# Unread matrix products in TensorE's waits, and weight remainders moved forward on VectorE, in a two-layer attention and expert kernel

## The chip, the cores and the metric

The kernel runs on one core of one Trainium2 chip. The time is device microseconds of one execution of the whole program, lower is better. The time before is the median of three runs, 1602.66 us (1599.79, 1602.66 and 1603.99).

## The reference, cut to what matters

4096 tokens (4 sequences of 1024) of 128 features pass through four blocks, each followed by a residual and a layer norm:

```python
x = _layernorm(x + _L0_attn_ref(x, ...))   # causal attention, 16 heads of 8, scores clipped to +-10
x = _layernorm(x + _L0_ffn_ref(x, ...))    # 8 experts, top 2: (silu(x W1) * (x W2)) W3, width 256
x = _layernorm(x + _L1_attn_ref(x, ...))   # full attention, 16 heads of 8, rotary embedding
x = _layernorm(x + _L1_ffn_ref(x, ...))    # 4 experts, top 2: gelu(x We1) We2, width 512
```

All of it is float32. Every expert is computed for every token and weighted by its gate.

## The kernel before

The five engines run their own programs and meet only at semaphores. The order of the stages is fixed: q, k and v of layer 0 (to about 31 us), causal attention of layer 0 (`pe_causal`, to about 301 us), the experts of layer 0 (`pe_end(.., 0)`, to about 702 us, which also makes q, k and v of layer 1), full attention of layer 1 (`pe_full`, to about 1357 us), the experts of layer 1 (`pe_end(.., 1)`).

**Experts of layer 0.** Tokens come in eight chunks of 512 (`CH`). A chunk has 16 steps (`SPC`). The work that prepares a chunk, its "front" (output projection, residual, norm, transposes, router), and the work that finishes one, its "back" (norm, rotation, q, k, v of layer 1), are spread over the steps beside the expert matmuls; the table `plan` says at which step each piece stands. For layer 0 the front's pieces are `o_turn` and `o_proj` at 1, `norm` at 3, `x_turn` at 4, `router` at 5. The very first front has no expert matmuls beside it: `pe_end`, `act_end` and `dve_end` call the 16 steps alone. In it VectorE divides the attention output by the row sums (`ot`, L1377), takes a reciprocal (L553), adds the residual (L1384), takes the statistics (L1284, L1287); GpSimd makes `rstd` of them with two small operations (L1518, L1519); VectorE normalises (`xs`, L1292); TensorE transposes `xs` (L946); ScalarE copies the result twice (`xt`, L1209, and its rounded half `x_hi`, L1210); TensorE computes the router (L1102), VectorE the remainder `x_lo` (L1401). Then the first expert matmuls start (L1031).

Float32 is made of rounded halves in the expert matmuls: a weight `w` is `w_hi + w_lo`. ScalarE rounds (`w_hi`, `w3_hi`), VectorE subtracts: `w_lo[0]` and `w_lo[1]` (L1486) after step `norm`, and `w3_lo` (L1490) after all 16 steps. `pe_first_hidden` waits for `w_lo`, `x_lo` and then `w3_lo`.

**The last back and the start of the full attention.** After the last chunk, 16 steps of back alone run (`pe_beside(.., 2 * B - 1, None, ..)`), with eight "pairs" between them (`pe_pair_beside_back`). A pair is two matmuls of 32 contracted rows and 512 columns into one slot of a ring of two (`max_pair`, L689); VectorE takes their row maxima (`negmax_h`, L808) and frees the slot. `pe_full` then issues pairs 8 to 27 alone (`first_pairs`), eight score matmuls (L703), and 16 rounds of 16 steps. A step has two parts, each with one pair, two scores and four value matmuls of 256 columns (`full_o`, L718); a score waits until ScalarE's exponential (L771) has emptied one of three banks.

Of the kernel before, what the change touches and what calls it, by code (L numbers as in the profile page):

```python
# [7 lines left out]
ALU = mybir.AluOpType  # L8
# [198 lines left out]
def build_program(nc, d, out):  # L207
    with ExitStack() as ctx:
# [548 lines left out]
        def pe_full(pe, L):  # L757
            for m in first_pairs(L):
                pe_pair(pe, L, 0, 0, m, m, m % 2)
            for e in range(HG * AHEAD):  # L760
                pe_score(pe, L, 0, 0, e)
            pe_full_round(pe, L, 0, 0, True)
            for i in range(1, NG):
                pe_full_round(pe, L, i, i % 2, i < NG - 1)
# [237 lines left out]
        EARLY_STEPS = {s: [n] for s, n in zip(EARLY, (plan[1].o_proj, plan[1].x_turn, plan[1].hidden, plan[1].router))}  # L1002
        RH_AT = 8
        n_exp = [E0, E1]

# [132 lines left out]
        def pe_chunk(pe, st, c, par, back, front, layer):  # L1138
            for n in range(SPC):
# [8 lines left out]
                pe_product(pe, st, c, n, layer)  # L1148

        def pe_first_hidden(pe, st, layer):  # L1150

            pe.wait_ge(w_lower, 2 * (layer + 1))
            for n in range(h_lead[layer]):
                pe_hidden(pe, st, 0, 0, n, layer)
            if layer == 0:
                pe.wait_ge(st.w3_lower, 1)
# [9 lines left out]
        def pe_end(pe, st, layer):  # L1166
            if layer == 0:
                for n in range(SPC):
                    pe_beside(pe, st, n, None, 0, 0, layer)
            else:  # L1170
                pe.wait_ge(st.gate_pre, 1)
# [6 lines left out]
            for n in range(SPC):  # L1178
                pe_beside(pe, st, n, 2 * B - 1, None, 0, layer)
                if layer == 0:  # L1180
                    pe_pair_beside_back(pe, layers[1], n)

# [287 lines left out]
        def dve_end(dve, st, layer):  # L1471
# [4 lines left out]
            for n in range(SPC):  # L1476
                dve_beside(dve, st, n, None, 0, 0, layer)
                if layer == 1 and n == plan[1].x_turn:
                    for k in range(2):
                        dve.wait_ge(raw_loaded[k], 32)  # L1480
                        nc.vector.tensor_copy(w_hi[k][:, :], w_raw[k][:, :]).then_inc(w_upper, 1)
                if n == (plan[0].norm, plan[1].x_turn)[layer]:

                    for k in range(2):
                        dve.wait_ge(w_upper, 2 * layer + k + 1)
                        nc.vector.tensor_tensor(w_lo[k][:, :], w_raw[k][:, :], w_hi[k][:, :].bitcast(F32),  # L1486
                                                ALU.subtract).then_inc(w_lower, 1)
            if layer == 0:
                dve.wait_ge(st.w3_upper, 1)
                nc.vector.tensor_tensor(w3_lo[:, :, :], w3[:, :, :], w3_hi[:, :, :].bitcast(F32),  # L1490
                                        ALU.subtract).then_inc(st.w3_lower, 1)
                dve.wait_ge(rope_loaded, 16 * 2)
# [359 lines left out]
```

## Time and profile before

| What | Value |
|---|---|
| median of three runs | 1602.66 us |
| profiled execution, its own time | 1611.3 us |
| its span, first to last instruction | 1609.5 us |
| TensorE busy | 1471.5 us (91%) |
| VectorE busy | 1400.4 us (87%) |
| ScalarE busy | 1202.9 us (75%) |
| mean granted TensorE clock | 0.952 |

### The profile page before, as it was taken

How to read it: one execution, taken by the hardware profiler on the slowest of the kernel's cores; microseconds unless marked ns; L12 is line 12 of the kernel's file. 1: busy time of each engine (PE TensorE's matmuls, PEld its weight loads, DVE VectorE, ACT ScalarE, POOL GpSimd, SP SyncE). 2: the span in 40 equal slices, each digit the busy share in tenths (PEclk: the TensorE clock that was granted, in tenths of full speed). 3: DMA queues.
4: the chain of work that ended last, by engine and by line, in shares of the span. 5: the costliest groups of instructions: out<-in, count | busy, mean ns of one | idle time of the engine just before them, and what ended most of it. 6: DMA issues, size and time to landing. Idle time of an engine off the chain costs nothing.

```text
span 1609.5 us, 32282 instructions
## 1 busy us (share of the span) xinstructions
PE 1471.5 (91%) x11200; PEld 797.1 (50%) x11200; DVE 1400.4 (87%) x2394; ACT 1202.9 (75%) x1897; POOL 307.5 (19%) x325
## 2 busy tenths in 40 slices
PE   7989898689999999969999999999999998999996
PEld 4333333377777777623333333333333334777775
DVE  5899999878888988887999999999999973788886
ACT  4999999644445454417999999999999986777775
POOL 0000000234455454420000000000000001234333
PEclk9899999799999998966999999999999997999999
DMA  6636432131224431111111111111111110211211
GB/s 203 203 106 182 120 102 86 49 107 40 96 93 127 128 108 66 66 41 51 46 37 37 46 45 38 42 37 36 37 36 36 37 32 28 69 56 63 75 56 40
DMA packets 71026, 116.76 MB, mean 73 GB/s; under 512 B 23808, under 2 KB 33920, under 8 KB 70272
## 3 DMA queue, kind: packets, MB, share of 16 engines
q1 hardware_dynamic: 70912, 115.21, 23.5%
q8 instruction: 75, 1.23, 0.3%
q14 instruction: 39, 0.32, 0.1%
HBM read 73.49 MB, written 41.16 MB: 71 GB/s over the span
## 4 chain that ended last, share of the span: by engine, by line
PE 61%; DVE 15%; ACT 10%; issue 10%; POOL 1%; DMA 1%; DVEq 0%; ACTq 0%; SPq 0%; POOLq 0%
PE full_o L718 14%; PE hid_pair L1031 12%; PE max_pair L689 11%; ACT cprobs L491 7%; PE bank L1134 7%; DVE negmax_h L808 5%; PE score L703 4%; PE causal_o L463 3%; PE triple L447 2%; PE bank L1066 2%; ACT o_sb L779 1%; DVE st L1284 1%; PE hid_pair L952 1%; PE bank L1094 1%; DVE hid_lo L1458 1%
## 5 line engine op out<-in xcount | busy, mean ns | idle before, releaser
L771 ACT ACTIVATE probs<-score 128x512 f32<-128x512 f32 x1024 | 546.6, 596 | 89.5 <-PE score L703 69.5
L808 DVE TENSOR_REDUCE negmax_h<-max_pair 128x2 f32<-128x1024 f32 x512 | 588.6, 1216 | 24.9 <-PE max_pair L689 24.8
L718 PE MATMUL full_o<-probs,v_st 128*32 128x256 f32 x4096 | 337.9, 403 | 17.7 <-ACT o_sb L779 17.7
L703 PE MATMUL score<-q_st,k_st 32*128 32x512 f32 x1024 | 319.9, 510 | 2.6 <-ACT probs L771 2.6
L689 PE MATMUL max_pair<-k_st,q_st 32*128 32x512 f32 x1024 | 264.7, 515 | 12.2 <-DVE negmax_h L808 10.8
L491 ACT ACTIVATE cprobs<-triple 128x1536 f32<-128x1536 f32 x192 | 258.4, 1713 | 5.2 <-PE triple L447 5.2
L689 PEld LDWEIGHTS max_pair<-k_st,q_st 32*128 32x128 f32 x1024 | 97.8, 188 | 236.7 <-DVE negmax_h L808 179.9
L1240 ACT ACTIVATE act_s<-hid_pair 128x512 f32<-128x512 f32 x128 | 76.7, 599 | 149.5 <-PE hid_pair L1031 149.5
L1031 PE MATMUL hid_pair<-x_hi,w_hi 128*128 128x512 f32 x384 | 171.3, 446 | 1.8 <-DVE x_lo L1401 1.0
L521 DVE TENSOR_SCALAR cprobs<-cprobs 128x1536 f32<-128x1536 f32 (+6 forms) x272 | 160.7, 618 | 2.9 <-ACT cprobs L491 2.9
L463 PE MATMUL causal_o<-cprobs,v_st 128*32 128x512 f32 (+3 forms) x1536 | 156.2, 502 | 2.2 <-DVE cprobs L521 2.2
L718 PEld LDWEIGHTS full_o<-probs,v_st 128*32 128x32 f32 x4096 | 83.3, 109 | 150.0 <-issue 94.5
L703 PEld LDWEIGHTS score<-q_st,k_st 32*128 32x128 f32 x1024 | 141.6, 187 | 28.8 <-ACT probs L771 19.5
L1031 PE MATMUL hid_pair<-x_lo,w_hi 128*128 128x512 f32 x384 | 154.6, 403 | 0.0
L1031 PE MATMUL hid_pair<-x_hi,w_lo 128*128 128x512 f32 x384 | 154.3, 402 | 0.0
L447 PE MATMUL triple<-q_st,k_st 32*128 32x512 f32 (+3 forms) x768 | 101.5, 429 | 28.7 <-ACT cprobs L491 26.0
L447 PEld LDWEIGHTS triple<-q_st,k_st 32*128 32x128 f32 x768 | 47.6, 186 | 135.5 <-ACT cprobs L491 127.1
L1248 ACT ACTIVATE hid_hi<-hid_pair,be 128x512 fp32r<-128x512 f32 x128 | 89.0, 695 | 24.9 <-PE hid_pair L1031 17.9
L1134 PE MATMUL bank<-hid_hi,w_hi 128*128 128x512 f32 x256 | 101.9, 398 | 1.4 <-DVE qk_lo L1436 1.3
L1134 PE MATMUL bank<-hid_hi,w_lo 128*128 128x512 f32 x256 | 101.4, 396 | 0.0
L568 POOL COPY v_st<-v_all 128x256 f32<-128x256 f32 x32 | 12.7, 400 | 434.6 <-PE causal_o L463 246.3
L520 DVE SCALAR_TENSOR_TENSOR cprobs<-cprobs,bound 128x256 f32<-128x256 f32 (+4 forms) x160 | 92.3, 577 | 3.9 <-ACT cprobs L491 2.5
(157 smaller groups left out, 2001.8 us busy)
## 6 DMA issues: line engine op xcount, KB each, us to landing
gate_all<-gate_scr SPq DMA_DIRECT2D x48, 512.0 KB, 4.3
o_scr<-o_sb SPq DMA_DIRECT2D x64, 256.0 KB, 2.1
k_st<-k_scr SPq DMA_DIRECT2D x64, 128.0 KB, 2.8
q_st<-q_scr SPq DMA_DIRECT2D x128, 64.0 KB, 2.5
k_st<-k_scr SPq DMA_DIRECT2D x64, 96.0 KB
q_st<-q_scr SPq DMA_DIRECT2D x64, 96.0 KB
q_scr<-qk_hi SPq DMA_DIRECT2D x18, 256.0 KB, 4.6
k_scr<-qk_hi SPq DMA_DIRECT2D x18, 256.0 KB, 4.5
```

The costliest lines, as they stand in the source:

```text
L447: last = nc.tensor.matmul(triple[n % 2][:, bk, off:off + w], k_st[p][rows, kt * P:(kt + 1) * P], q_st[p][rows, q0:q0 + w], start=True, sto ...
L463: last = nc.tensor.matmul(causal_o[qc][SLOT * j:SLOT * (j + 1), c0:c0 + w], v_st[p][:, kt, j, :], cprobs[at % CP][:, bk, off:off + w], sta ...
L491: nc.scalar.activation(cprobs[n % CP][:, :, :], triple[n % 2][:, :, :], ACT.Exp, scale=SCALE).then_inc(L.exp_done, 1)
L520: nc.vector.scalar_tensor_tensor(edge, edge, float(np.exp(-CLIP)), limit, ALU.max, ALU.min)
L521: ins = nc.vector.tensor_scalar(plain, plain, float(np.exp(-CLIP)), float(np.exp(CLIP)), ALU.max, ALU.min)
L689: last = nc.tensor.matmul(ring[slot][:, k, :], q_st[p][rows, qt * P:(qt + 1) * P], k_st[p][rows, half * CH:(half + 1) * CH], start=True, s ...
L703: nc.tensor.matmul(sbank[L.score_bank(e)][:, :], k_st[p][rows, kt * P:(kt + 1) * P], q_st[p][rows, q0:q0 + w], start=True, stop=True, tile ...
L718: last = nc.tensor.matmul(full_o[SLOT * j:SLOT * (j + 1), cols], v_st[p][:, kt, j, :], probs[s % NP][:, j, cols], start=(kt == 0 and part ...
L771: nc.scalar.activation(probs[s % NP][:, L.HEADS[j], :], sbank[L.score_bank(e)][:, :], ACT.Exp, scale=SCALE).then_inc(L.exp_done, 1)
L808: nc.vector.tensor_reduce(negmax_h[:, qt // TPC, half, heads[0]:heads[1] + 1:2, qt % TPC], ring[slot][:, :, :], AXX, ALU.max, negate=True) ...
L1031: last = nc.tensor.matmul(hbank[2 * k + n % h_banks[layer]], w[:, slice_of(n)], x[:, :], start=(a == 0), stop=(a == 2))
L1134: last = nc.tensor.matmul(y_bank[e % 2], w, x, start=(f == 0 and a == 0), stop=(f == per - 1 and a == 2))
```

## The change

A helper issues products that nobody reads: the 128x128 identity times the first columns of the table `rope_a`, float32. They are put at five places in TensorE's program: one of 512 columns at the start of the first front, three after its step 1, one after its step 4; two after step 1 and two after step 2 of the last back; one of 256 columns after each of the 20 pairs of `first_pairs`. On VectorE, `w_lo[0]` is computed after step 0 of the first front (behind `ot` and the reciprocal), `w_lo[1]` after step 1 (behind the statistics), `w3_lo` after step 3 (behind `xs`).

```diff
@@ pe_full
             for m in first_pairs(L):
                 pe_pair(pe, L, 0, 0, m, m, m % 2)
+                pe_keep_busy(bank[0], 1, CH // 2)
@@
+        BUSY_FRONT, BUSY_BACK = {1: 3, 4: 1}, {1: 2, 2: 2}
@@
+        def pe_keep_busy(to, many, cols):
+
+            for _ in range(many):
+                nc.tensor.matmul(to[:, 0:cols], ident[:, :], rope_a[:, 0:cols], start=True, stop=True)
@@ pe_end
             if layer == 0:
+                pe.wait_ge(rope_loaded, 16 * 2)
+                pe_keep_busy(hbank[0], 1, CH)
                 for n in range(SPC):
                     pe_beside(pe, st, n, None, 0, 0, layer)
+                    if n in BUSY_FRONT:
+                        pe_keep_busy(hbank[0], BUSY_FRONT[n], CH)
@@
                 if layer == 0:
                     pe_pair_beside_back(pe, layers[1], n)
+                    if n in BUSY_BACK:
+                        pe.wait_ge(st.v_saved, 2 * B - 1)
+                        pe_keep_busy(bank[2], BUSY_BACK[n], CH)
@@ dve_end
-                if n == (plan[0].norm, plan[1].x_turn)[layer]:
-
-                    for k in range(2):
+                if layer == 0 and n == plan[0].norm:
+                    dve.wait_ge(st.w3_upper, 1)
+                    nc.vector.tensor_tensor(w3_lo[:, :, :], w3[:, :, :], w3_hi[:, :, :].bitcast(F32),
+                                            ALU.subtract).then_inc(st.w3_lower, 1)
+                for k in ((0,) if n == plan[0].o_turn - 1 else (1,) if n == plan[0].o_proj else ()) if layer == 0 else (
+                        (0, 1) if n == plan[1].x_turn else ()):
                         dve.wait_ge(w_upper, 2 * layer + k + 1)
                         nc.vector.tensor_tensor(w_lo[k][:, :], w_raw[k][:, :], w_hi[k][:, :].bitcast(F32),
                                                 ALU.subtract).then_inc(w_lower, 1)
             if layer == 0:
-                dve.wait_ge(st.w3_upper, 1)
-                nc.vector.tensor_tensor(w3_lo[:, :, :], w3[:, :, :], w3_hi[:, :, :].bitcast(F32),
-                                        ALU.subtract).then_inc(st.w3_lower, 1)
                 dve.wait_ge(rope_loaded, 16 * 2)
```

## Rows read from the trace of the kernel before

**Rows 1.** One piece of the chain that ended last (start us, us, what).

```profile
699.81 12.46 DVE negmax_h L808 x11
```

**Rows 2.** Timeline of VectorE in the first front (start us, length us, engine, line).

```profile
301.92 0.55 DVE L553 RECIPROCAL s_rcp<-s_raw 128x64 f32<-128x64 f32 x1
304.70 0.69 DVE L1384 TENSOR_TENSOR res<-x_tm,bank 128x512 f32<-128x512 f32 x1 [2.24 <-PE bank L1082]
...
306.44 0.38 DVE L1287 BATCH_NORM_AGGREGATE mv<-st 128x2 f32<-128x6 f32 x4
308.48 1.11 DVE L1292 TENSOR_SCALAR xs<-res,mv,rstd 128x128 f32<-128x128 f32 x4 [1.66 <-POOL rstd L1519]
309.51 4.49 DVE L1486 TENSOR_TENSOR w_lo<-w_raw,w_hi 128x2048 fp32r<-128x2048 f32 x2
313.91 0.68 DVE L1401 TENSOR_TENSOR x_lo<-xt,x_hi 128x512 fp32r<-128x512 f32 x1
...
316.36 2.28 DVE L1490 TENSOR_TENSOR w_lo<-w,w_hi 128x2048 fp32r<-128x2048 f32 x1
```

**Rows 3.** Timeline of GpSimd, in the first front and in the chunk after it.

```profile
307.40 1.04 POOL L1519 TENSOR_TENSOR rstd<-rstd,mhalf 128x4 f32<-128x4 f32 x1
316.52 2.99 POOL L1542 TENSOR_TENSOR p<-euler,lead 128x4 f32<-128x4 f32 x1 [8.07 <-DVE lead L1303]
...
343.44 1.02 POOL L1542 TENSOR_TENSOR p<-euler,lead 128x4 f32<-128x4 f32 x1 [2.71 <-DVE lead L1303]
```

**Rows 4.** Timeline of TensorE: float32 products of 512 columns at full clock, then the first front.

```profile
17.03 1.88 PE L952 MATMUL hid_pair<-xt,w_qkv 128*128 128x512 f32 x4
...
302.14 2.04 PE L1082 MATMUL bank<-w_o,ot 128*128 128x128 f32 x8 [1.50 <-DVE ot L1377]
309.65 1.12 PE L946 MATMUL bank<-ident,xs 128*128 128x128 f32 x4 [5.46 <-DVE xs L1292]
312.03 1.85 PE L1102 MATMUL bank<-wg,xt 128*128 128x8 f32 x8 [1.27 <-ACT x_hi L1210]
```

**Rows 5.** TensorE by stretch in the first front: length, busy us, granted clock, DMA share, GB/s.

```profile
306.00:310.00 4.00, 0.35 (x2) 0.50 0.42 131
...
314.85:318.80 3.95, 3.95 (x9) 0.50 0.00 0
```

**Rows 6.** TensorE by stretch, last back to full attention: length, busy us, granted clock.

```profile
701.40:704.80 3.40, 1.50 (x8) 1.00 0.00 0
704.80:723.90 19.10, 12.77 (x34) 0.50 0.28 85
...
729.60:756.00 26.40, 26.40 (x181) 0.50 0.01 2
...
760.00:1300.00 540.00, 522.67 (x5472) 1.00 0.15 42
```

**Rows 7.** Timeline of TensorE: q and k of the last back, a pair of `first_pairs`.

```profile
691.59 3.47 PE L1066 MATMUL bank<-xt,w_qkv 128*128 128x512 f32 x4 [0.69 <-ACT xt L1194]
...
702.13 0.50 PE L689 MATMUL max_pair<-k_st,q_st 32*128 32x512 f32 x2 [0.64 <-DVE negmax_h L808]
```

**Rows 8.** VectorE's maxima from 699.7 to 726.2 us, grouped: count, busy us, mean ns.

```profile
L808 DVE TENSOR_REDUCE negmax_h<-max_pair 128x2 f32<-128x1024 f32 x23 | 26.2, 1216 | 0.0
```

**Rows 9.** Timeline of TensorE: a part of attention at half clock, then one at full clock.

```profile
730.62 0.79 PE L689 MATMUL max_pair<-k_st,q_st 32*128 32x512 f32 x2
...
731.35 1.08 PE L718 MATMUL full_o<-probs,v_st 128*32 128x256 f32 x8
732.36 0.79 PE L689 MATMUL max_pair<-k_st,q_st 32*128 32x512 f32 x2
...
758.52 0.50 PE L689 MATMUL max_pair<-k_st,q_st 32*128 32x512 f32 x2
...
759.53 0.50 PE L689 MATMUL max_pair<-k_st,q_st 32*128 32x512 f32 x2
```

**Rows 10.** Timeline of ScalarE: the first exponentials of the full attention.

```profile
725.24 5.13 ACT L771 ACTIVATE probs<-score 128x512 f32<-128x512 f32 x10 [21.42 <-PE score L703]
```

## The prediction

> **What bounds the kernel now.** I read the page first: a span of 1609.5 us, with TensorE 91% and VectorE 87% busy (the table above), so neither has much room on average and the question is which waits the edits touch. The mean granted clock of 0.952 says that some 155 us ran at 1.2 GHz (0.048 of the span is missing, and each us at the other level, half, misses half of itself). Most of TensorE's work sits at full clock, so I then cut the span into stretches by the granted clock. The reader is to see two things there. In the first front TensorE is nearly idle and the clock is at 0.50, and it is still 0.50 while the first expert matmuls run back to back [rows 5]. And from 704.8 to 756 us it is at 0.50 in one piece: 19 us in which TensorE issues lone pairs, 5.7 us of scores, and 26.4 us of attention in which it never rests [rows 6]. The same attention work runs at 1.00 for the 540 us behind it [rows 6].
>
> The chain of waits then says who sets the time in these stretches. In `first_pairs` it is VectorE: its maxima stand in the chain one after the other [rows 1], 23 of them in 26.2 us with no idle time [rows 8], so 1.13 to 1.14 us for each. TensorE's pair takes 0.50 us at full clock and then sits idle 0.64 us until a slot is free [rows 7]. In the attention behind it TensorE sets the time while the clock is low: a part takes 732.36 - 730.62 = 1.74 us at half clock and 759.53 - 758.52 = 1.01 us where nothing holds it at full clock [rows 9]; there VectorE's 1.135 us is the longer [rows 8]. A part at half clock thus costs 1.74 - 1.135 = 0.6 us. 26.4 us hold 15 of them: 9.1 us.
>
> In the first front the timelines show one chain: statistics, `rstd` on GpSimd, `xs`, transpose, ScalarE's copies, then `x_lo` on VectorE, which stands behind the two `w_lo` [rows 2], then the first expert matmul at 314.85 us, the start of the second stretch of [rows 5].
>
> **The change part by part.**
>
> *One product's price.* Two float32 products of 512 columns take 1.88 us at full clock [rows 4], so 0.94 us alone and, back to back, a little less; at half clock two take 3.47 us [rows 7], 1.74 us each. One of 256 columns is half of that plus its start.
>
> *The first front on VectorE.* `w_lo[0]` takes 4.49 / 2 = 2.25 us. It starts behind the reciprocal, at about 302.4, and ends at 304.65; the residual started at 304.70 [rows 2]. It fits to 0.05 us and costs nothing; it also uses up what a faster projection (2.04 us at half clock [rows 4]) could have given. `w_lo[1]` starts right behind the statistics at about 306.75 and ends at 309.0. VectorE would have been free for `xs` at 308.48, so by VectorE alone this costs 0.5 us. But GpSimd works on `rstd` in just that time. The trace shows what that does: L1542 takes 1.02 us in one chunk and 2.99 us in the one where it starts 0.16 us after VectorE's 2.28 us `w3_lo` [rows 2, 3]; it ends 0.87 us behind that operation's end, as if it had only begun then. `w_lo[1]` is the same kind, a subtraction of two SBUF tensors of 2048 columns, and starts before GpSimd's first operation. So I take `rstd` to be held until 309.0, plus about 0.1 and 1.04 us [rows 3]: `xs` starts at 310.2, 1.7 us late. Bounds: 0.5 and 1.9 us late.
>
> The Trainium skill, "GPSIMD Engine Reference", section Key points, says that GpSimd shares its SBUF interfaces with VectorE and contends with VectorE instructions that have two SBUF inputs. By that rule the delay is 1.7 us, without it 0.5; the 2.99 us row agrees with the rule.
>
> Behind `xs`: transpose 311.4 to 312.5 at half clock [rows 4], `x_hi` ready about 313.6, `w3_lo` 311.3 to 313.5 in cover of these, `x_lo` done by 314.3. That part alone would be a gain, since `x_lo` started at 313.91 before [rows 2]. TensorE, however, has its own new product after the transpose: 1.74 us at half clock, to 314.2; the router needs 1.85 us more [rows 4], to 316.0. The first expert matmul starts at 316.0 against 314.85: +1.1 us. Lower bound: if `rstd` isn't held, router and product end at 314.8, 0 us. If the clock were still full here, the router would end by 314.2 and the expert matmuls start at 314.5, 0.3 us early, and their first 18 would run at full clock: up to 2.5 us gained. I don't take it: the products after step 1 end by 302.14 + 1.0 + 3 x 0.9 = 305.8, and from there to 311.4 TensorE has nothing; the row of an idle stretch like it is at 0.50 [rows 5]. **Front: +1.1 us, -2.5 to +1.5.** `w3_lo` no longer stands at 316.36, where it held VectorE until the moment ScalarE's first output was there; that removal frees nothing else.
>
> *The last back.* Four products of 512 columns stand in TensorE's waits from 681 to 687 us, at step 1 and 2. The semaphore they wait for (the seventh v) was raised a chunk earlier. Behind them stand pair 2, which nobody reads before 689.6, and the transposes; a product at full clock ends well ahead of both. Gain: the transposes and perhaps the start of q and k at full clock, at most half of 3.47 us, likely 0.5 us. **Back: -0.5 us, -2 to 0.**
>
> *`first_pairs`.* 20 products of 256 columns. Here the clock decides the sign. The trace has no product behind a pair, but four value matmuls of 256 columns stream as long as such a product and stand behind a pair in the same way [rows 9]. At full clock that makes 1.01 us against VectorE's 1.13: hidden, by 0.12 us. At half clock it makes 0.73 + 1.01 = 1.74 us, and TensorE becomes the bound: 0.6 us lost at each pair, 12.1 us over 20. Nor does this work bring the clock back: the attention at half clock has the same rhythm with more in it, without a pause, and stayed at 0.50 for 26.4 us [rows 6]. So what is the clock when the loop is entered? In the profiled execution it is 1.00 until 704.8, three pairs in, after a stretch with only 1.50 us of work in 3.40 [rows 6]. The stretch ahead of the first pairs (waits for the rotation) gets no product. It is as likely to fall there, a pair or two earlier than in the profile, as to be caught by the products. I take 14 pairs at half clock, near the 17 that the profile had: 14 x 0.6 = 8.5 us; ends 0 and 12.1.
>
> *The start of the attention.* Even where the loop keeps the clock, TensorE then has eight scores, paced by ScalarE at 0.51 us each [rows 10]: 4 to 5 us with no product in them, each score of 32 rows only. It is thinner work than the pairs beside which the clock fell [rows 6]. I therefore take the 26.4 us of slow attention to stay as they are.
>
> **Sum.** +1.1 - 0.5 + 8.5 = +9.1 us. The profiled execution took 1611.3 us, 8.6 above the median of the runs; its long stretch of slow attention (9.1 us) may well be shorter in others, and the loop's loss doesn't depend on it. Added to the median 1602.66: **1612 us**, own range 1606 to 1619.
>
> **The rivals.**
>
> *A: the products carry the clock through the loop and the scores.* Then the attention starts at 1.00 and up to 15 parts run in 1.135 us: -9.1 us in the profiled execution, some 7 in one at the median, since the two differ by 8.6 us; with -0.5 and +1.1: 1596 us (1592 to 1600). For it: at full clock the loop with products has TensorE working 1.01 us in 1.13, more than any stretch before which the clock fell. Against it: the wait of the scores, and the entry. It decides if the clock is full at 702 us and doesn't fall between the last pair and the first values. The clock fell in the middle of pairs, with idle gaps of only 0.6 us between them [rows 6, 7]. The Trainium skill, "TensorE: Matmul & The Clock Gate", section "What's actually happening", says that the default is the throttled state and activity releases it; section "Why this matters for your kernels" advises against long idle gaps alone. By that rule the loop, the scores and the attention, which have no long gap once the products are in, keep the full clock, and the time is A's; the pairs beside which the clock fell had no long gap either, so the trace doesn't bear the rule out for such thin work. Chance 0.33.
>
> *B: no effect on the bound.* The clock is full in the loop, whose products are hidden, and falls in the scores; the attention starts slow as before. -0.5 + 1.1 = +0.6: 1603 us (1599 to 1607). The lengthening of the slow attention by chance counts here too. Chance 0.22.
>
> *C: the forecast*, half clock in the loop, TensorE the bound. Chance 0.45.
>
> **How the numbers follow.** A change under 0.3% (4.8 us; the three runs lie 4.2 apart) can't be told from none. C gives slower but for a few of its cases with few slow pairs (0.04), A faster but for as many, B mostly same. Faster 0.34, same 0.22, slower 0.44. The range must take in A and C: 1593 to 1618.
>
> **What would show it.** Right: a granted clock of 0.50 in the loop, products and pairs 1.7 us apart, VectorE idle between the maxima for the first time; `rstd` (L1518 with L1519) ending near 310.1 and `xs` starting near 310.2; the first expert matmul near 316. Wrong: clock 1.00 from 702 us to beyond 730, maxima still 1.13 us apart, and attention parts of 1.14 us from the first. If the clock falls between 725 and 730 and the total is unchanged, B is right. The prediction fails above all if the clock tolerates thin score work, or if the products of the last back carry it over the waits for the rotation.

## The result, and the profile after

The changed kernel took 1627.2 us (median of 4 runs, 1620.93 to 1632.45) against 1603.3 us before (1599.79 to 1606.55): a ratio of 1.014, with a 95% interval of 1.010 to 1.018. In a second comparison, on other runs, it was 1.010 (1.008 to 1.012). The change makes the kernel 17 to 24 us slower. 1612 us was forecast and 1618 was the end of the range. The direction and the place were right, the size was not. The profiled execution took 1632.45 us, the slowest of the four, with a span of 1630.7 us; its counterpart before took 1611.3 us.

The loop of `first_pairs` comes first. The timeline of TensorE of the changed kernel there, answering to [rows 7] (L689 is a pair, L1155 a product of 256 columns, L703 a score):

```profile
702.26 0.49 PE L689 MATMUL max_pair<-k_st,q_st 32*128 32x512 f32 x2 [0.63 <-DVE negmax_h L809]
702.68 1.11 PE L1155 MATMUL bank<-rope_a,ident 128*128 128x256 f32 x2
703.72 0.79 PE L689 MATMUL max_pair<-k_st,q_st 32*128 32x512 f32 x2
704.44 1.22 PE L1155 MATMUL bank<-rope_a,ident 128*128 128x256 f32 x2
705.59 0.79 PE L689 MATMUL max_pair<-k_st,q_st 32*128 32x512 f32 x2
...
737.44 0.79 PE L689 MATMUL max_pair<-k_st,q_st 32*128 32x512 f32 x2
738.16 1.22 PE L1155 MATMUL bank<-rope_a,ident 128*128 128x256 f32 x2
739.31 0.80 PE L703 MATMUL score<-q_st,k_st 32*128 32x512 f32 x3
```

Only the first pair still waits for VectorE. From 703.72 to 737.44 us there are 18 equal steps of 33.72 / 18 = 1.87 us, each one a pair (0.72 us until the product starts) and a product (1.15 us until the next pair starts), and a last product delays the first score. VectorE is the one that waits now (its maxima from 702 to 739 us, grouped, answering to [rows 8]; the last columns are its idle time and what ended it):

```profile
L809 DVE TENSOR_REDUCE negmax_h<-max_pair 128x2 f32<-128x1024 f32 x22 | 26.8, 1224 | 11.4 <-PE max_pair L689 11.3
```

The chain that ended last says the same: in this stretch it has none of VectorE's maxima as a long piece, as [rows 1] had. The first line is its shares of the stretch from 702 to 745 us.

```profile
by line: PE bank L1155 53.3%; PE max_pair L689 33.1%; PE score L703 10.7%; DVE negmax_h L809 2.7%; ACT probs L772 1.4%; PE full_o L718 1.3%; issue 0.2%
...
704.51 1.15 PE bank L1155 x2
```

TensorE by stretch, answering to [rows 6] (length, busy us of PE, PEld, DVE, ACT and POOL, granted clock, DMA share, GB/s):

```profile
696.00:702.80 6.80, 4.56 (x21) 2.33 (x22) 5.79 (x7) 2.09 (x4) 4.05 (x4) 1.00 0.01 2
702.80:739.30 36.50, 36.50 (x78) 15.18 (x78) 25.05 (x23) 1.14 (x2) 2.03 (x5) 0.50 0.14 44
744.50:771.10 26.60, 26.60 (x185) 7.81 (x188) 18.31 (x17) 16.04 (x30) 0.42 (x2) 0.50 0.01 3
771.10:1300.00 528.90, 511.50 (x5356) 200.14 (x5352) 514.87 (x502) 486.48 (x920) 17.26 (x70) 1.00 0.15 43
```

The clock is full until 702.80 us, while the loop's first product (from 702.68 us) runs. Then it is at half, 1.2 GHz, for the rest of the loop, though TensorE is busy in all of the 36.50 us. Before, the same 20 pairs ran from 702.13 to the first score at 723.94 us. The attention behind it is slow for as long as before (26.6 us against 26.4).

The first front: VectorE's timeline, answering to [rows 2], then GpSimd's [rows 3] and TensorE's [rows 4].

```profile
302.18 2.23 DVE L1503 TENSOR_TENSOR w_lo<-w_raw,w_hi 128x2048 fp32r<-128x2048 f32 x1
304.33 0.67 DVE L1398 TENSOR_TENSOR res<-x_tm,bank 128x512 f32<-128x512 f32 x1
...
306.35 2.26 DVE L1503 TENSOR_TENSOR w_lo<-w_raw,w_hi 128x2048 fp32r<-128x2048 f32 x1
309.85 1.11 DVE L1306 TENSOR_SCALAR xs<-res,mv,rstd 128x128 f32<-128x128 f32 x4 [1.25 <-POOL rstd L1533]
...
313.29 0.69 DVE L1415 TENSOR_TENSOR x_lo<-xt,x_hi 128x512 fp32r<-128x512 f32 x1
```

```profile
306.70 1.99 POOL L1532 TENSOR_SCALAR rstd<-mv 128x4 f32<-128x4 f32 x1 [7.51 <-DVE mv L1301]
308.78 1.04 POOL L1533 TENSOR_TENSOR rstd<-rstd,mhalf 128x4 f32<-128x4 f32 x1
```

The first of these two operations in the kernel before, from its timeline of GpSimd:

```profile
307.09 0.23 POOL L1518 TENSOR_SCALAR rstd<-mv 128x4 f32<-128x4 f32 x1 [7.70 <-DVE mv L1287]
```

```profile
311.02 1.12 PE L947 MATMUL bank<-ident,xs 128*128 128x128 f32 x4 [5.43 <-DVE xs L1306]
311.93 1.92 PE L1155 MATMUL hid_pair<-rope_a,ident 128*128 128x512 f32 x2
313.64 1.71 PE L1104 MATMUL bank<-wg,xt 128*128 128x8 f32 x8
315.21 0.77 PE L1033 MATMUL hid_pair<-x_hi,w_hi 128*128 128x512 f32 x1
```

GpSimd's first `rstd` operation takes 1.99 us instead of 0.23 us where VectorE's `w_lo[1]` runs beside it, and ends 0.08 us behind that one. The first expert matmul starts at 315.21 us, 0.36 us later than in [rows 5]. From 311.02 us until then TensorE has no idle time.

Where the 21.2 us between the two profiled spans lie, by stage (distances between the same instructions in the two timelines):

| stage | before | after | difference |
|---|---|---|---|
| start to the loop's first pair | 702.1 | 702.3 | +0.1 |
| the loop, to the first score | 21.8 | 37.0 | +15.2 |
| scores, to the first values | 5.7 | 5.3 | -0.4 |
| first round of attention | 47.3 | 47.3 | 0.0 |
| rounds 2 to 15 | 531.5 | 531.5 | 0.0 |
| last round, to layer 1's first expert matmul | 49.2 | 53.3 | +4.1 |
| experts of layer 1, to the end | 251.9 | 254.1 | +2.2 |

### The profile page after: what moved, and what is told of

Its sections match the earlier page's. It is cut to its first block, busy times and chain, and to the rows that moved or that the text cites. A ratio compares the mean times of both kernels' runs of the same rounds, so it can differ in the third digit from the quotient of the medians.

```text
span 1630.7 us, 32398 instructions
## 1 busy us (share of the span) xinstructions
PE 1503.6 (92%) x11258; PEld 809.2 (50%) x11258; DVE 1405.9 (86%) x2394; ACT 1203.3 (74%) x1897; POOL 306.5 (19%) x325
## 4 chain that ended last, share of the span: by engine, by line
PE 61%; DVE 15%; issue 11%; ACT 10%; POOL 1%; DMA 1%; DVEq 0%; ACTq 0%; SPq 0%; POOLq 0%
PE full_o L718 14%; PE hid_pair L1033 12%; PE max_pair L689 11%; ACT cprobs L491 7%; PE bank L1136 7%; DVE negmax_h L809 4%; PE score L703 4%; PE causal_o L463 3%; PE bank L1068 2%; PE triple L447 2%; PE bank L1155 1%; ACT o_sb L780 1%; DVE st L1298 1%; PE hid_pair L953 1%; PE bank L1096 1%
## 5 line engine op out<-in xcount | busy, mean ns | idle before, releaser
L703 PE MATMUL score<-q_st,k_st 32*128 32x512 f32 x1024 | 320.5, 513 | 2.6 <-ACT probs L772 2.6
L689 PE MATMUL max_pair<-k_st,q_st 32*128 32x512 f32 x1024 | 265.6, 515 | 2.6 <-DVE negmax_h L809 1.2
L689 PEld LDWEIGHTS max_pair<-k_st,q_st 32*128 32x128 f32 x1024 | 98.0, 188 | 231.2 <-DVE negmax_h L809 161.7
L703 PEld LDWEIGHTS score<-q_st,k_st 32*128 32x128 f32 x1024 | 142.0, 187 | 30.4 <-ACT probs L772 20.8
L447 PEld LDWEIGHTS triple<-q_st,k_st 32*128 32x128 f32 x768 | 47.3, 185 | 135.3 <-ACT cprobs L491 125.9
L1262 ACT ACTIVATE hid_hi<-hid_pair,be 128x512 fp32r<-128x512 f32 x128 | 88.9, 694 | 24.7 <-PE hid_pair L1033 17.4
```

The source lines that it names most:

```text
L447: last = nc.tensor.matmul(triple[n % 2][:, bk, off:off + w], k_st[p][rows, kt * P:(kt + 1) * P], q_st[p][rows, q0:q0 + w], start=True, sto ...
L689: last = nc.tensor.matmul(ring[slot][:, k, :], q_st[p][rows, qt * P:(qt + 1) * P], k_st[p][rows, half * CH:(half + 1) * CH], start=True, s ...
L703: nc.tensor.matmul(sbank[L.score_bank(e)][:, :], k_st[p][rows, kt * P:(kt + 1) * P], q_st[p][rows, q0:q0 + w], start=True, stop=True, tile ...
```

## The experiments

Each ratio is against the kernel before in the same comparison, whose median lay between 1605.4 and 1608.0 us in the four sets. "Loop" is from the loop's first pair to the first score (21.8 us before, 37.0 after), "last round" from the start of the last round of the attention to layer 1's first expert matmul (49.2 and 53.3), "front" from the last causal matmul to layer 0's first expert matmul (14.5 and 15.0).

### The parts of the change, one by one

**e1_loop_only** is before with only this (and the function that it calls):

```diff
             for m in first_pairs(L):
                 pe_pair(pe, L, 0, 0, m, m, m % 2)
+                pe_keep_busy(bank[0], 1, CH // 2)
```

> The kernel before with one edit of the change: the 20 products of 256 columns behind the pairs of the loop. Theory 1 (the loop at half clock is the whole loss): the trace of the changed kernel has 1.87 us from pair to pair against 1.13, so 20 pairs give +14.8 us, about 1618 us and up to 1627 if the chance part of the changed kernel's loss is in it too; the granted clock is 0.50 in nearly all of the loop. Theory 2 (the loop is only part, the front's products and the moved subtractions hold the rest): 1612 to 1618 us and the kernel without these 20 products still 5 to 9 us above before.

Measured: 1627.4 us, 1.0133 (1.010 to 1.016), loop 37.4 us, last round 58.7. The loop's products alone cost as much as the whole change. In this profile the clock fell as the loop was entered (699.9 us), so all 20 pairs ran at half clock.

**e2_no_loop** is the changed kernel without that line.

> The changed kernel without the 20 products in the loop; all else of the change stays. Theory 1: the loss is gone, within 2 us of the kernel before (-1 to +2). Theory 2: still 5 to 9 us slower. First expert matmul about 0.4 us later than in the kernel before relative to the end of the causal attention, as in the changed kernel; maxima again 1.13 us apart.

Measured: 1610.3 us, 1.0026 (1.001 to 1.004), loop 21.8 us, last round 49.8. Without the loop's products 17 us of the changed kernel's 1627 are gone. What is left is still slower than before by 4 us (1.4 to 6.9), more than the 2 us that theory 1 allowed, and the next three runs find it in neither part of the rest; it stays open.

**e3_vector_order** is before with only VectorE's three subtractions moved as in the change. **e14_front_only** is the front with its products as well, **e15_back_only** the last back's four products alone.

> The kernel before, with only VectorE's three subtractions of the first front moved as in the change, and no product. Theory 1, GpSimd's rstd is held by the moved subtraction: xs starts near 309.9 us instead of 308.5, but without the product ahead of the router TensorE has its operands 1 us earlier than in the changed kernel: from the last causal matmul to the first expert matmul 13.6 to 14.3 us, the total within 1 us of before. Theory 2, the hold of GpSimd is what costs: 15 us from the last causal matmul to the first expert matmul, as in the changed kernel (15.0), and the total 1 to 2 us above before.

> The change's front alone: VectorE's order and the five products of the first front, nothing in the last back or the loop. Front and back together stood 4.2 us above before, VectorE's order alone 0.3. Theory 1, the front costs what its stretch shows: from the last causal matmul to the first expert matmul 14.4 to 15.0 us against 13.6 to 14.5 without it, +1 us, a total of +0.5 to +1.5. Rival, the 4.2 us stand in the front: +3 to +5 in all, with something behind the front longer too.

> The change's four products in the last back alone. The prediction had -0.5 us (-2 to 0). Theory 1: between -1.5 and +1 us in all; the first 8 pairs at the same place as before within 1 us. Rival, the products let the clock be full for q and k but fall in the rotation behind them, so that the loop and the attention behind it run at half clock longer: +2 to +4.

| | us | ratio | front | start to the loop's first pair |
|---|---|---|---|---|
| e3_vector_order | 1607.4 | 1.0002 (0.9986 to 1.0018) | 14.9 | 701.4 |
| e14_front_only | 1608.0 | 1.0007 (0.9990 to 1.0025) | 15.0 | 701.9 |
| e15_back_only | 1605.2 | 0.9994 (0.9978 to 1.0011) | 13.6 | 699.9 |

None can be told from before. In the order-only kernel GpSimd's `rstd` is held in the same way, with no product anywhere. Its timelines of GpSimd and of VectorE, one row each:

```profile
307.05 2.00 POOL L1518 TENSOR_SCALAR rstd<-mv 128x4 f32<-128x4 f32 x1 [7.93 <-DVE mv L1287]
```

```profile
306.70 2.26 DVE L1489 TENSOR_TENSOR w_lo<-w_raw,w_hi 128x2048 fp32r<-128x2048 f32 x1
```

So the front's price is VectorE's order and not the product ahead of the router: 14.9 us without it, 15.0 with it. Of the ten profiles with the old front eight have 13.6 us (the profile of before, with 14.5, and e4's, with 14.2, are the exceptions), and the eight with the new one have 14.4 to 15.0. So the new front costs 0.8 to 1.5 us against those eight, close to the +1.1 of the sum, by another path. Theory 1 of the order-only run was wrong in this stretch: the delay isn't absorbed without the product. The totals are too close to tell its two theories apart.

Three of the seven profiles with the front's products (e2, e5 and e11, those with 14.4 us) show that they can raise the clock of the matmuls behind them. There the clock was at half only for 3.4 us, from about 311 us, and the second router came 24.7 to 24.9 us after the first; in the four others it was at half for 10.2 us, and the distance was 26.8 to 27.8 us. With the old front the clock fell between 302.1 and 305.0 us, with these products between 308.4 and 311.1.

### The size of the products

**e6_loop_64** is the changed kernel with `CH // 8` (64 columns) in the loop.

> The changed kernel with the loop's products of 64 columns in place of 256. At half clock the pair's 0.73 us and a product of a quarter of the length, some 0.3 to 0.45 us, stay near VectorE's 1.13 us. Theory 1: pairs 1.13 to 1.2 us apart, within 3 us of before. If the cost is in the product's start and not in its columns: pairs about 1.4 us apart or more, +5 us and over.

Measured: 1612.8 us, 1.0045 (1.003 to 1.007), loop 26.2 us. TensorE's timeline, at half clock:

```profile
706.34 0.79 PE L689 MATMUL max_pair<-k_st,q_st 32*128 32x512 f32 x2
707.06 0.69 PE L1155 MATMUL bank<-rope_a,ident 128*128 128x64 f32 x2
707.67 0.79 PE L689 MATMUL max_pair<-k_st,q_st 32*128 32x512 f32 x2
```

A step takes 1.34 us on average, still longer than VectorE's 1.13. The product takes 0.61 us of it with a quarter of the columns; 192 more columns cost 0.54 us. If the cost grows evenly with the columns, the part that doesn't depend on them is 0.43 us (an estimate from these two sizes), over a third of the 1.15. The result lies between the two cases of the expectation.

### The same delay without products

**e10_plain_delay** gives VectorE the delay instead:

```diff
             for m in first_pairs(L):
+                qt, half, heads = pair_of(m)
+                dve.wait_ge(L.ring_ready, m + 1)
+                nc.vector.tensor_reduce(spare[:, m, :],
+                                        ring[m % 2][:, :, 0:328], AXX, ALU.max, negate=True)
                 dve_pair(dve, L, m, m, m % 2)
```

> The kernel before, without any product, but with each of the 20 maxima of the loop preceded by a second maximum over 328 of the 512 columns, into a tile of its own: about 0.74 us more of VectorE for each pair, the delay that the products at half clock brought. Theory 1, the loss is the loop's length and nothing else about the products: pairs 1.87 us apart, loop +15 us, and the total 1617 to 1621 as far as the rest behind the loop is chance, or 1625 to 1629 if whatever delays the loop also lengthens the stages behind it. Theory 2, TensorE's products themselves change the later clock: the total is +15 here and +22 with the products alone.

Measured: 1618.9 us, 1.0065 (1.004 to 1.009), loop 35.3 us (pairs 1.88 us apart), last round 47.7. A loop 13.5 us longer costs 10.5 us in all (6 to 14). So most or all of a delay there reaches the end, and it doesn't draw the later stages out with it. The loop's products cost 21 us (17 to 26) in e1, clearly more than that delay, and 14 us (9 to 18) in e9 (below), which can't be told from it. 0.7 to 2.2 us of the difference stand in the loop itself (36.0 to 37.5 us with products).

### The clock at the entry

**e5_full_entry** is the changed kernel with products of 512, 512, 256 and 128 columns in the waits for the rotation (steps 4, 7, 8 and 9 of the last back), so that the loop is entered at full clock:

```diff
+        BUSY_ROT = {4: CH, 7: CH, 8: CH // 2, 9: CH // 4}
...
+                    if n in BUSY_ROT:
+                        pe_keep_busy(bank[0], 1, BUSY_ROT[n])
```

> The changed kernel with more unread products ahead of the loop: one of 512 columns after steps 4 and 7 of the last back, one of 256 after step 8 and one of 128 after step 9, so that TensorE has work in the waits for the rotation. It asks what the products in the loop do if the loop is entered at full clock. If thin scores let the clock fall (rival B of the prediction): clock 1.00 in the loop, maxima 1.13 us apart, clock 0.50 again by about 730 us, time within 3 us of before (1600 to 1607). If the products carry it through (rival A): clock 1.00 throughout, attention parts 1.14 us apart from the first, 1594 to 1599 us. If the entry still falls to half: 1618 to 1630 us as the changed kernel.

Measured: 1606.5 us, 1.0014 (0.999 to 1.0035), loop 22.9 us. TensorE's timeline and its stretches:

```profile
700.35 0.50 PE L689 MATMUL max_pair<-k_st,q_st 32*128 32x512 f32 x2 [0.21 <-DVE negmax_h L809]
700.77 0.70 PE L1156 MATMUL bank<-rope_a,ident 128*128 128x256 f32 x2
701.48 0.49 PE L689 MATMUL max_pair<-k_st,q_st 32*128 32x512 f32 x2
...
724.44 2.45 PE L703 MATMUL score<-q_st,k_st 32*128 32x512 f32 x5 [0.74 <-ACT probs L772]
```

```profile
700.35:723.20 22.85, 22.45 (x81) 9.62 (x81) 22.82 (x23) 1.66 (x3) 2.58 (x6) 1.00 0.23 71
723.20:727.60 4.40, 3.66 (x13) 1.56 (x12) 1.59 (x3) 3.81 (x8) 0.00 (x0) 1.00 0.00 0
727.60:734.40 6.80, 6.80 (x49) 1.89 (x48) 4.34 (x4) 4.45 (x9) 0.00 (x0) 0.50 0.01 2
```

This run tells the rivals apart. The same 20 products at full clock leave the pairs 1.13 us apart: hidden, as the prediction had it, but for the last one, which holds the first score back by 1.0 us. The loop's loss is thus a matter of the clock in it, and that is decided by the work ahead of it, not by the clock at its first pair: the changed kernel too entered it at full clock, but the clock fell 0.5 us later, and in its second profile (e11) 2.3 us later, beside two pairs with their products. The 6.80 us ahead of the first pair, first in e11, then in this run:

```profile
691.00:697.80 6.80, 4.18 (x20) 2.02 (x19) 5.79 (x8) 1.57 (x3) 3.51 (x3) 1.00 0.01 2
693.55:700.35 6.80, 6.28 (x28) 2.92 (x26) 5.79 (x8) 1.57 (x3) 3.51 (x3) 1.00 0.01 2
```

TensorE was busy for 4.18 us of them there and for 6.28 us here. In all three kernels with products in the waits for the rotation (this one, e13 and e16) the clock stayed full through the loop. It falls at 727.6 us, between the first scores and the first values: rival B's picture. It stands 17 to 21 us below the changed kernel, and not below before.

**e13_carried** (before with the products of the last back, the rotation and the loop, none behind the last pair, and with 128 columns behind each of the five scores that wait for ScalarE) asks whether denser scores keep the clock.

> The kernel before with products in the last back (the change's four of 512 columns, and 512, 512, 256 and 128 columns in the waits for the rotation), in the loop behind each pair but the last, and of 128 columns behind each of the five scores that wait for ScalarE; the front as before. With full_entry the clock was 1.00 through the loop and fell at 727.6 us in the scores. Theory 1, denser scores keep it: no half clock between 696 us and the last round, the first round 37.9 to 39 us instead of 40.6 and 47.3, and a total of 1598 to 1603. Rival, the scores of 32 rows still let it fall: half clock from about 728 us, the first round above 40 us, and the total within 2 us of before.

Measured: 1612.9 us, 1.0051 (1.003 to 1.007). The loop is back at 21.8 us, but the clock fell all the same:

```profile
700.70:722.50 21.80, 21.43 (x77) 9.15 (x78) 21.77 (x22) 1.66 (x3) 2.58 (x6) 1.00 0.24 74
722.50:726.90 4.40, 3.66 (x15) 1.91 (x15) 2.21 (x2) 3.26 (x6) 0.00 (x0) 1.00 0.00 0
726.90:747.40 20.50, 20.50 (x134) 6.68 (x137) 12.55 (x12) 12.05 (x22) 0.42 (x2) 0.50 0.02 3
```

TensorE is busy for 3.66 of the 4.40 us ahead of the fall in both kernels. The rival of that run is right about the clock: it falls in the scores, with or without products between them, and so it did in e16 below (720.9 us, scores from 719.2). It is wrong about the total, which is 8 us above before: the stretch from the first score to the first values is 1.6 us longer (7.3 against 5.7), and the last round took 53.6 us.

**e4_dense_start** puts a product of 128 columns ahead of each pair in the first four steps of the attention's first round, where the clock is at half; the loop is as before.

> The kernel before, with a product of 128 columns in the ring slot ahead of each pair in the first four steps of the first round of the second layer's attention; the loop is left alone. At half clock a part there is bound by TensorE (1.74 us), so each product adds some 0.6 us to about 16 parts unless the clock rises. Theory 1, denser work brings the clock back earlier: the rise comes 10 us or more before 756 us, and the total is 2 to 5 us below before. Rival, TensorE's work there is already without a pause, so more of it changes nothing in the clock: the slow stretch stays as long or becomes longer, and the total is 2 to 8 us above before.

Measured: 1617.9 us, 1.0065 (1.004 to 1.009). The clock rose at 746.8 us, 9 us earlier than in the profile of before, but in the other kernels whose loop is as before it rose between 737.0 and 748.4 us as well. The first round took 46.9 us, against 43.8 to 44.3 in e7, e8 and e15, whose clock was at half in it for about as long (16 to 17 us). The products delay a stretch that TensorE sets and bring nothing that can be seen.

### What lies behind the loop

e1 and the changed kernel lose more than their loops. In e1's last round TensorE waited 1.44 us for GpSimd's `ot` (0.38 before), and the clock fell right behind it for 23.9 us, and once more later. **e8_last_round** (before) and **e9_loop_and_last_round** (e1) have two products of 512 columns behind step 8 of the last round, where TensorE stands still for 1.85 us in the kernel before. **e11_after_again** is the changed kernel once more, **e12_after_last_round** the changed kernel with those two products.

> The kernel before, with two products of 512 columns (on w_qkv1 instead of rope_a, whose memory is in use by then) behind step 8 of the last round of the second layer's attention, where TensorE stood still from 1333.9 to 1336.04 us and the clock fell to 0.50 at 1336.3 for 20.5 us. Theory 1, the clock falls there because of that gap: it stays at 1.00, or falls later, and the stretch from the start of the last round to the first expert matmul of layer 1 shrinks from 49.2 us to some 43 to 46: -3 to -6 us in all. Rival, the scarce work of TensorE around the early front lets it fall anyway: 49 to 50 us, and the total within 1 us of before.

> The loop's products alone, and the two products in the last round as well. The loop alone cost 22 us at the median, of which 15.6 stood in the loop; the profile showed 9.5 us more in the last round and 2.3 in the experts behind it. Theory 1, the rest above 15.6 is slow clock in the last round: with the products there this kernel stands 15 to 17 us above the one with the last round's products alone. Theory 2, the rest lies elsewhere or falls by chance: 20 to 24 us above it, and the last round takes anything from 49 to 59 us.

> The changed kernel once more, for a second profile and more times, since its +24 us at the median holds 15 us of loop and some 8 that its profile showed in other places (the last round of the second layer's attention 53.3 us against 49.2, the experts of layer 1 254.1 against 251.9). Theory 1, these are chance of where the clock falls in one execution: the loop again 37.1 us, but the last round 47 to 50 us, and a total of 1619 to 1624. Theory 2, they belong to the change: the last round is again above 52 us, and the total 1625 to 1632.

> The changed kernel with the two products of 512 columns behind step 8 of the last round as well. Theory 1, TensorE's gap in the last round is where the rest of the loss arises: 4 to 8 us below the changed kernel, as the loop's products with these products stood 14.8 us above before, and those without 22.0. Rival, they do nothing here either, as alone (0.3 us below before): within 2 us of the changed kernel.

| | us | ratio | loop | first round | last round |
|---|---|---|---|---|---|
| e8_last_round | 1607.6 | 0.9988 (0.9970 to 1.0006) | 21.8 | 44.3 | 50.0 |
| e9_loop_and_last_round | 1622.8 | 1.0086 (1.0058 to 1.0115) | 37.5 | 44.8 | 47.3 |
| e11_after_again | 1623.9 | 1.0102 (1.0083 to 1.0122) | 36.0 | 43.8 | 54.7 |
| e12_after_last_round | 1626.4 | 1.0133 (1.0109 to 1.0157) | 36.0 | 41.4 | 49.8 |

The two products do nothing alone: in e8 TensorE still waited 1.02 us behind them, and the clock fell there for 20.5 us as before. The pair e8 and e9 differs by 15.2 us, just the loop's 15.6; but with them the changed kernel isn't faster (e12 against e11), so theory 1 of that run falls. The changed kernel's second profile (e11) has a long last round again, as its theory 2 said, though its total is theory 1's. A row of TensorE's timeline in e1's last round, with its wait, and then e9's last round as a stretch, at a granted clock of 0.89 (before 0.79):

```profile
1323.99 1.54 PE L1083 MATMUL hid_pair<-w_o,ot 128*128 128x128 f32 x8 [1.44 <-POOL ot L1560]
```

```profile
1317.80:1365.20 47.40, 44.08 (x353) 18.75 (x353) 20.86 (x53) 33.74 (x62) 5.84 (x6) 0.89 0.09 25
```

Two things vary in these stages: how late the sums come back through memory (in e1 SyncE waited 3.2 us for `s_rcp`'s transfer, before 1.3), and how long the clock is at half. The second sets the length of the last round: over all 18 profiles it goes from 47.3 us with 10.2 us at half clock (e9) over 48.8 to 50.1 with 20.5 to 58.7 with 44.4 (e1), some 0.36 us for each us at half. Around the gap at step 8 the clock fell in every profile but e9's and e12's, two of the three kernels with products ahead of that gap, where it fell 6.6 and 9.8 us behind it. What the long rounds have more is an early fall. It came 17.5 to 19.5 us into the round in the changed kernel, e6, e11, e12 and e13, and in each of these TensorE waited there 1.17 to 1.60 us for VectorE's `xs`; e16 waited 1.16 us without a fall, and in all others that wait was 0.77 us or less. e1 fell earlier still, behind the wait for `ot`. The row of the changed kernel:

```profile
1340.92 0.97 PE L947 MATMUL hid_pair<-ident,xs 128*128 128x128 f32 x4 [1.17 <-DVE xs L1306]
```
Over all profiles the last round took 47.3 to 58.7 us (mean 52.7) in the six kernels whose loop was slowed by products, and 47.7 to 50.1 in eleven of the twelve others, 53.6 in e13. That looks like more than chance, by some 3 us, but no run shows what would carry it over the 580 us between the loop and this round; it stays open. The +2.2 us of layer 1's experts in the table above is no such sign: that stage took 251.3 to 254.5 us in the kernels without a slowed loop.

### Is there a place where the products pay?

**e7_chunk_waits** puts two products of 512 columns into layer 0's chunks, behind the statistics, where TensorE waits for the normalised tokens and the clock fell for 3.4 us or more in each chunk. **e16_waits_and_full_entry** joins them to e13's products, without those behind the scores.

```diff
                 if n == pl.x_turn:
+                    if layer == 0 and front > 0:
+                        pe.wait_ge(st.stats, front + 1)
+                        pe_keep_busy(bank[2], 2, CH)
                     pe.wait_ge(st.norm, front + 1)
```

> The kernel before, with two products of 512 columns in each chunk of layer 0's experts, where TensorE waits for the normalised tokens of the next chunk (behind the statistics). Before shows seven stretches of 3.4 to 10 us at half clock there, 30.7 us in all, so at most 15 us of TensorE's work. Theory 1, the gap at that wait lets the clock fall and TensorE sets the chunk's time: fewer such stretches, the experts of layer 0 5 to 10 us shorter, a total of 1595 to 1601. Rival, the products run into the time of the matmuls behind them, or the stretches lie in cover of VectorE: the total within 2 us of before or above it.

> The products in the waits of layer 0's chunks together with those of the last back, of the waits for the rotation and of the loop (not behind its last pair), the front as before. Theory 1: what the chunk waits give, and 2 us less than full_entry, which had the front's products as well (+1.0 against before): 1593 to 1600. Rival: neither part gives anything by itself, 1605 to 1610.

Measured: 1610.3 us, 1.0019 (1.0003 to 1.0035), and 1607.9 us, 1.0010 (0.999 to 1.0025). The clock did fall less often: in e7 the chunks from 366 to 407, 448 to 489 and 530 to 571 us ran at 1.00 throughout, all of them at 0.96 before. The half-clock stretches of layer 0's chunks add up to 20.5 us in e7 and 13.7 in e16, against 30.7 in before (23.9 to 30.7 in the kernels without these products), and the kernel isn't faster. The first row is e7's, the second that of before:

```profile
366.00:407.00 41.00, 38.60 (x177) 29.25 (x176) 35.91 (x87) 19.66 (x36) 19.59 (x16) 1.00 0.17 48
```

```profile
366.00:407.00 41.00, 38.07 (x172) 29.51 (x172) 35.93 (x87) 20.00 (x36) 21.39 (x17) 0.96 0.23 77
```

The distances from router to router say why. From the third router to the seventh they are 45.65, 46.92, 45.84 and 46.74 us in before, with four half-clock stretches of 3.4 us in them, and 45.83, 46.70, 46.03 and 46.68 us in e7, with two: 185.1 and 185.2 us in all, so the chunks take such a stretch up. Only a longer one costs. Where the clock was at half for 10.2 us around the second router (e7 itself, e13 and e15) the distance from there to the third is 42.5 to 42.7 us instead of 40.3 to 40.6, and e6 and e8, with 10.2 us at half around the sixth, have 48.9 instead of 46.7 from there to the seventh.

No version of the products beats the kernel before.

## Why the prediction was wrong in size

**The clock at the entry: left open, and its number a compromise.** "It is as likely to fall there ... as to be caught by the products": it fell at 702.8 us, one pair into the loop, and in e1 with the first pair. That part of C's case came true, but it had been given no more than even odds. The products of the last back kept it full for q and k in e15 (where before had 10.2 us at half), but not for the loop: e15 entered it at 699.9 us and fell at 702.2 all the same.

**The loop: the step that failed.** "14 x 0.6 = 8.5 us; ends 0 and 12.1", for 14 pairs at half clock. The mechanism was right, the term was sized too small. Both factors were low. 19 of the 20 pairs ran at half clock (18 to 20 in the other profiles with these products), since the clock fell at 0 to 2.3 us into the loop and nothing in it brought it back. And a step took 1.87 us, not 1.74: the pair 0.72 as in the sum, the product 1.15 instead of 1.01. I had taken the product from four value matmuls of 256 columns that use a 32-column tile each [rows 9]; a product over the full array costs 0.14 us more behind a pair. Worked out again: 18 steps x 0.74 = 13.4, 0.3 for the first step, and 1.9 because the first score, which used to start beside the last pair, now waits for that pair and its product, which the sum left out; less 0.3 that two of before's steps had been longer by. That is 15.3 us, and the two timelines differ by 15.2. Even the end of 12.1 us lay below it. With 15.2 in place of 8.5 the forecast would have been 1618 us, still 9 us below the median of the four runs; for what is missing the sum had no term (below).

**Nothing raises the clock in the loop: right.** 36.5 us of TensorE without a pause stayed at 0.50. The Trainium skill, "TensorE: Matmul & The Clock Gate", section "What's actually happening", says that activity releases the throttled state; the stretch of 36.50 us busy in 36.50 at 0.50 doesn't bear that out for this mixture, while the full entry shows that the same mixture keeps a clock that is full.

**The front: right in GpSimd and near in size, wrong in its last link.** `rstd` ended at 309.8 us (310.1 forecast), `xs` started at 309.85 (310.2), the first expert matmul at 315.21 (316.0). The Trainium skill, "GPSIMD Engine Reference", section Key points, has GpSimd contend with VectorE's instructions of two SBUF inputs; the 1.99 us of L1532 and the 2.00 us in the order-only run agree. The price comes from that hold and not from the product ahead of the router. The products did move the clock's fall, from 302.1 us before to 310.3. The prediction took it to come ahead of the transposes at 311 us, and so it did here, but only just; the gain of up to 2.5 us that it named and didn't take is about what e2, e5 and e11 show (24.7 to 24.9 us to the second router instead of 26.8 to 27.8).

**The last back: not contradicted.** -0.5 us (-2 to 0) forecast, a ratio of 0.9994 measured, so -1.0 us with an interval of -3.5 to +1.8. In the changed kernel's own profile its mechanism didn't work: the clock fell at 689.2 us all the same, and the first four records of q and k took 3.78 us at half clock, against 3.47 before [rows 7].

**The attention behind it: right, for another reason and with some luck.** Rival A didn't happen, and the clock fell in the scores even where the loop had run at full clock. But the prediction called the scores "thinner work than the pairs", and by the share of busy time they aren't: 3.66 of 4.40 us in e5, against 1.50 of 3.40 us for the pairs beside which the clock fell [rows 6]. That the slow stretch stayed as long as before (26.6 and 26.4 us) is luck too: in the other profiles 3.4 to 18.6 us of the first round were at half clock, 15.7 us in the same kernel's second profile (e11), and before and the changed kernel are the two longest.

**What the sum had no term for:** 3 to 9 us beyond the loop. The profile shows 6.3, in the last round and in layer 1's experts. The 2.2 us of the experts are within what that stage varies by. The 4.1 of the last round come from a second stretch at half clock behind a wait of 1.17 us for `xs`; why the kernels with a slowed loop have it more often is open, and so are the 4 us of e2.

## What to carry to other kernels

Work that is added to keep TensorE's clock up has to be priced at half clock too, since a clock that has already fallen turns it from cover into the bound. Here the same 20 products cost 1 us at full clock and 15 at half, and what TensorE did ahead of the loop decided which: with products in the waits ahead of it the clock stayed full, without them it fell in the first 2.7 us. Price such a product from a row of the same tile shape, and count its fixed part (by the estimate above 0.43 us at half clock), which doesn't shrink with the columns.

A higher clock is worth something only where TensorE's slower work reaches the next wait: three stretches of 41 us of the experts at 1.00 instead of 0.96 left the routers as far apart as before, while stretches of 10.2 us at half clock cost 2 us each.

## What the runs showed of the hardware

The same pairs and products have no clock of their own: they ran at 0.50 for 36.5 us in the changed kernel, without a pause, and at 1.00 for 22.85 us in e5 (22.45 us busy). Both were at 1.00 at the first pair; they differ in the work ahead of it. In the full attention the clock rose, after 6.8 us at half in e5 and with the attention's first 26.4 us behind it in before, during the same work.

The fall in the scores came behind 3.66 us of work in 4.40, with and without products between them; before's loop fell behind 1.50 us in 3.40 [rows 6]. The scores use 32 of the 128 rows, but no run changed the rows alone, so whether that is why isn't shown.

An operation of GpSimd that takes 0.23 us alone (L1518 at 307.09 us in before) takes 1.99 us beside VectorE's subtraction of two SBUF tensors, and 2.00 us in the order-only kernel: it ends 0.08 to 0.09 us behind the subtraction.
